# Order of VectorE's work in a 72-job dense stage: normalise early, fill the row table in the first attention, spread the kept folds

## The reference, cut to what matters

```python
x = x + attention(layernorm(x))                       # first attention
m = gelu(layernorm(x) @ w1 + b1) @ w2 + b2            # MLP
x = layernorm(x_in + x + m)
logits = einsum('bld,ed->ble', x, gate_weight)
kth_val = sort(logits.reshape(-1))[4 * 128 * 6 - 1]
gates = logits * (logits >= kth_val)
h = gelu(einsum('bld,ehd->bleh', x, w1) + b1)         # eight experts
out = einsum('blde,ble->bld', einsum('bleh,edh->blde', h, w2) + b2, gates)
x = layernorm(x + out)
```

## Time and profile before

| | |
|---|---|
| time, median of 3 runs | 1162.04 us (1162.0 to 1164.67) |
| profiled execution | 1153.58 us |
| its span, first to last instruction | 1151.9 us |
| mean granted TensorE clock | 0.922 |
| TensorE busy | 962.3 us, 84% |
| VectorE busy | 863.6 us, 75% |
| ScalarE busy | 741.1 us, 64% |
| GpSimd busy | 406.5 us, 35% |

### The profile page before, as it was taken

One profiled execution on the slowest core, in us unless ns is written; L12 is line 12 of the kernel. 1 busy time (PEld: TensorE's weight loads), 2 busy tenths in 40 slices (PEclk: granted clock), 3 DMA queues, 4 the chain that ended last, 5 costly groups with the idle time before them and its releaser, 6 DMA issues. The chain is left out here.

```text
span 1151.9 us, 29135 instructions
## 1 busy us (share of the span) xinstructions
PE 962.3 (84%) x10214; PEld 611.6 (53%) x10214; DVE 863.6 (75%) x2339; ACT 741.1 (64%) x1409; POOL 406.5 (35%) x572
## 2 busy tenths in 40 slices
PE   3999999946788999949889999589888861899995
PEld 2788887733444444414334444256565541689852
DVE  2899898836569999549899877558999864688833
ACT  2666666637688888828676788346555530688834
POOL 3455455434443000000100100113676677366643
PEclk9999999978799999979999999769989875899998
DMA  4000000010002999863222110100111101233244
GB/s 128 4 3 3 4 3 3 4 58 0 1 19 74 174 170 166 163 164 97 75 86 87 55 49 17 57 22 28 32 47 48 46 23 48 77 88 83 76 108 131
DMA packets 87997, 72.61 MB, mean 63 GB/s; under 512 B 8994, under 2 KB 73764, under 8 KB 87856
## 3 DMA queue, kind: packets, MB, share of 16 engines
q1 hardware_dynamic: 79088, 60.05, 23.1%
q0 software_dynamic: 4544, 8.60, 2.3%
q10 hardware_dynamic: 4224, 2.10, 0.7%
HBM read 40.14 MB, written 31.49 MB: 62 GB/s over the span
## 5 line engine op out<-in xcount | busy, mean ns | idle before, releaser
L778 ACT ACTIVATE d__hf<-d__HB,d__d 128x512 f32<-128x512 f32 x288 | 185.8, 681 | 76.2 <-PE d__HB L1001 72.1
L839 DVE TENSOR_TENSOR d__hl<-d__hf,d__hh 128x1024 f16<-128x1024 f32 x144 | 175.6, 1224 | 30.8 <-ACT d__hh L783 28.7
L783 ACT ACTIVATE d__hh<-d__hf 128x1024 f16<-128x1024 f32 x144 | 152.2, 1057 | 4.6
L751 POOL TENSOR_SCALAR d__rstd<-d__mv 128x4 f32<-128x4 f32 x16 | 15.0, 937 | 383.8 <-DVE d__mv L953 383.8
L999 PE MATMUL d__YB<-d__hh,d__w2h 128*128 128x512 f16 x288 | 110.3, 383 | 30.7 <-DVE d__hl L839 30.7
L999 PE MATMUL d__HB<-d__xh,d__w1h 128*128 128x512 f16 x288 | 114.2, 396 | 0.0
L1000 PE MATMUL d__HB<-d__xl,d__w1h 128*128 128x512 f16 x288 | 114.1, 396 | 0.0
L1001 PE MATMUL d__HB<-d__xh,d__w1l 128*128 128x512 f16 x288 | 113.1, 393 | 0.0
L1001 PE MATMUL d__YB<-d__hh,d__w2l 128*128 128x512 f16 x288 | 110.4, 383 | 0.0
L1000 PE MATMUL d__YB<-d__hl,d__w2h 128*128 128x512 f16 x288 | 110.3, 383 | 0.0
L298 POOL TENSOR_SCALAR_AFFINE_SELECT a__pt<-a__pt 128x512 f32<-128x512 f32 x128 | 81.6, 661 | 71.7 <-ACT a__pt L341 71.5
(11 more groups left out here) (376 smaller groups left out, 2532.9 us busy)
## 6 DMA issues: line engine op xcount, KB each, us to landing
rows<-d__blank SPq DMA_DIRECT2D x72, 268.0 KB, 7.6
d__G<-gates SPq DMA_DIRECT2D x64, 256.0 KB, 3.1
c__xin<-rows SPq DMA_DIRECT2D x39, 134.0 KB, 2.2
d__stage<-e_w SPq DMA_DIRECT2D x16, 256.0 KB, 3.2
b__stage<-e_w SPq DMA_DIRECT2D x32, 128.0 KB, 2.2
c__yb<-parts SPq DMA_DIRECT2D x8, 256.0 KB, 8.3
c__yb<-parts ACTq DMA_DIRECT2D x8, 256.0 KB, 8.8
out<-c__xo SPq DMA_DIRECT2D x8, 256.0 KB, 2.3
```

What stands on the lines that cost most here:

```text
L778: act.activation(hf[:, q, f], HB[:, f], gelu, scale=1.0 / WS, bias=b1[:, at:at + 1]).then_inc(s_["h_free"], 1)
L783: act.activation(hh[:, q, f - 1:f + 1], hf[:, q, f - 1:f + 1], ACT.Copy).then_inc(s_["hi_done"], 1)
L839: dve.tensor_tensor(hl[:, q, f], hf[:, q, f], hh[:, q, f], ALU.subtract).then_inc(s_["lo%d_done" % i], 1)
```

## The change

Three edits. (1) On VectorE in the dense stage hn(s+3) moves to the second place of the step, ahead of low(s,1), the statistics of job s+4 go ahead of xa, the first low weights go from step -4 to step -3 together with b2s and its wait for the small load. (2) The 72 writes of blank rows move to SP's queue in the first attention, five after each of its normalised blocks, from a tile with four rows for each partition instead of one row read four times. (3) The 22 kept results are folded at intervals of 9/5 steps, in steps 31 to 68, and each chunk has a sum of its own (eight tiles, not four).

```diff
@@ attention_0
+        blank = m.sb("blank", [P, 4, ROW])
+        blanks = rows.rearrange("(i p r) c -> p i r c", p=P, r=4)
...
             sp.dma_start(x[:, 4:NT, :], d["x"][:, 4:NT, :]).then_inc(x_rest, 16)
+            sp.wait_ge(blank_set, 1)
+            for i in range(BLANKS * NC_):
+                if i % 5 == 0:
+                    sp.wait_ge(hn_done, i // 5 + 1)
+                sp.dma_start(blanks[:, i], blank[:]).then_inc(blanked, 16)
+            sp.wait_ge(blanked, 16 * BLANKS * NC_)
...
             pool.wait_ge(cleared, 4)
+            pool.memset(blank[:], BLANK).then_inc(blank_set, 1)
             pool.wait_ge(loaded, 16 * LOADS)
@@ raw_pair(s)
-    i = s - FOLD_0
-    return M_JOBS + i if i >= 0 and kept_raw(M_JOBS + i) else None
+    for j in range(M_JOBS, FOLD_0):
+        if kept_raw(j) and FOLD_0 + (j - M_JOBS) * 9 // 5 == s:
+            return j
+    return None
@@ dense_0
-        acc = m.sb("acc", [P, 4, CT])
+        acc = m.sb("acc", [P, NC_, CT])
-        blank = m.sb("blank", [P, 1, ROW])
@@ dense_0, sync
-            sp.wait_ge(s_["blank_set"], 1)
-            for i in range(BLANKS * NC_):
-                if i % 4 == 0:
-                    sp.wait_ge(s_["counted"], min(i // 4 + 1, ROUNDS + 2))
-                sp.dma_start(blanks[:, i], blank[:].to_broadcast([P, 4, ROW])).then_inc(s_["blanked"], 16)
             sp.wait_ge(s_["gt_done"], 1)
@@ dense_0, vector
-            dve.wait_ge(s_["loaded"], 16)
-            dve.tensor_scalar(b2s[:], b2, WS, None, ALU.mult).then_inc(s_["b2_done"], 1)
...
+                c = s + 3
+                if 0 <= c < M_JOBS:
+                    if c:
+                        right_full(dve, "lift", c - 1)
+                    dve.wait_ge(s_["rstd0_done"], c + 1)
+                    for a in range(4):
+                        ins = dve.tensor_scalar(hn[:, a, :], x1[:, 4 * c + a, :], mv0[:, a, 0:1], rstd0[:, a:a + 1],
+                                                ALU.subtract, ALU.mult)
+                        ins.then_inc(s_["hn_done"], 1) if a == 3 else first.inc(ins)
                 if 0 <= s < JOBS:
                     low(s, 1)
...
                     left_full(dve, *post)
+                    wait(dve, s_["xn_done"], closed)
...
                 if 0 <= s + 1 < JOBS:
                     low(s + 1, 0)
-                if post:
-                    (the wait for rstd_done and xa)
-                c = s + 3
-                (hn(s + 3), as above)
                 c = s + 4
                 (statistics of job s + 4)
+                if post:
+                    (the wait for rstd_done and xa)
-                if s == BEGIN or 0 <= s - 5 < E:
-                    j = 0 if s == BEGIN else s - 4
+                if s == BEGIN + 1 or 0 <= s - 5 < E:
+                    j = 0 if s == BEGIN + 1 else s - 4
...
                     ins.then_inc(s_["w_done"], 1)
+                    if j == 0:
+                        dve.wait_ge(s_["loaded"], 16)
+                        dve.tensor_scalar(b2s[:], b2, WS, None, ALU.mult).then_inc(s_["b2_done"], 1)
```

## The result

The changed kernel took 1117.41 us (median of 4 runs, 1115.49 to 1118.96) beside 1162.3 for the kernel before in the same rounds (4 runs, 1162.0 to 1164.67): ratio 0.9623, 95% interval 0.959 to 0.9656. The forecast was 1121.2, in a range of 1111 to 1136. The profiled execution took 1118.96 us with a span of 1117.2, against 1153.58 and 1151.9 before. Some executions of a kernel fall into a slower group; ratios here compare the faster ones alone.

What follows compares the result with a forecast made beforehand. Bound taken: TensorE's own work plus three dense-stage losses (start and normalisation steps, one long stall, chunk-closing steps). Gains 17.0 + 19.8 + 4 = 40.8 us, then 0.7% from profile to median, gave 1121.2 us, range 1111 to 1136.

Steps and rivals of the forecast that it cites:

- Start and early steps: Dense stage up to job 7's first matmul: reordering VectorE's normalisation work gains 17.0 us, bounds 12 to 19.2.
- A(1): Start of L953, the bn_aggr of the job leaving the pipeline, in dense-stage step 1: forecast at 279.0.
- The loop: Dense-stage steps 2 to 4, from one bn_aggr start to the next: 9.85 us a step, with 0.83 for hn held.
- The end of 12 us: Lower bound of the early-step gain: two GpSimd xl instructions hold hn, or the lower clock hits a step without slack.
- Step 5: Early dense-stage step without hn: forecast 7.5 us.
- The stall: Wait before the first fold, gates queued behind SP's table writes: 24.94 us becomes 5.18, gain 19.8; 16 if landing takes twice as long.
- Rival 3: The stall at the first fold stays because gates to G is slow by itself: total gain 21.0, 1141; chance 0.04.
- The folds: Dense-stage steps 33 to 70: spreading kept folds cuts closing-step losses from 21.9 to 17.8 us; gain 4, bounds 0 and 9.
- the prediction's signs of being wrong: Attention ending after 250, early steps over 11 us, or the low clock coming back in the fold steps.
- Rival 2: Spread folds pile up at steps 57 to 59 and 65 to 69, fourth part loses 4: 1129.2; chance 0.1.
- The row table in the first attention: 72 writes, 19.8 MB, issued by SP on idle DMA engines: no effect taken; bounds -1 to +5 us.
- Rival 4: Slower than before: the table's writes slow the first attention, decisive from 40.8 us on; at 50% 1181; chance 0.03.

Runs made afterwards that it cites:

- after: The changed kernel with all three edits, as first measured and profiled: 1117.41 us, ratio 0.9623 to the kernel before.
- norm_table: The changed kernel without the third edit (first and second edits, folds one a step as before): 1116.83 us, ratio 0.967.
- table_only: The kernel before with only the second edit, the 72 row-table writes in the first attention: 1134.25 us, ratio 0.9823.
- norm_only: The kernel before with only the first edit, VectorE's new order; old table and folds: 1138.84 us, ratio 0.9879.
- after_third: The changed kernel, unedited, run again on the third chip: 1113.95 us, ratio 0.9674 to the kernel before.
- pool_waits: The changed kernel with GpSimd's two xl subtractions waiting until the next job's hn is done; second chip: 1146.64 us, ratio 0.9665.
- after_again: The changed kernel, unedited, run again on the second chip: 1151.2 us, ratio 0.9708 to the kernel before.
- low_first: The changed kernel with low(s,1) put ahead of hn(s+3) on VectorE; second chip: 1141.11 us, ratio 0.9654.
- waits_apart: The changed kernel with GpSimd's xl waiting for hn and kept folds neither in nor directly ahead of closing steps; third chip: 1103.62 us, ratio 0.955.
- apart: The changed kernel with the 22 kept folds moved out of the closing steps, these at least four apart; second chip: 1141.82 us, ratio 0.964.
- before_again: The kernel before, unedited, sent as an experiment on the third chip: 1150.37 us, ratio 0.9971.
- fold_only: The kernel before with only the third edit, kept folds every 9/5 steps and eight sums: 1149.71 us, ratio 0.9965.
- all_three: The changed kernel with xl waiting for hn, kept folds off closing steps, and low(s,1) ahead of hn(s+3); third chip: 1097.62 us, ratio 0.9513.

## Why the prediction was right

**Start and early steps: 17.0 forecast, 14.3 and 15.8 measured** (from the attention's end to job 7, in the two pairs of before and after; norm_table against table_only gives 16.7). The mechanism is right: norm_only shows it alone. A part of the gain comes through the clock: from job 0 to job 7 TensorE's own busy time fell by 4.8 us in the first pair and by 9.4 in the other (56.87 to 47.45), because less of it was at 1.2 GHz; no run separates this from the waits. The losses within it, in the first pair: *A(1)* was 283.17 and not 279.0. Of that the attention's later end is 2.3; hn(1), held by L749, 0.75; GpSimd's rstd0 under the second half of the low weights (L991) about 0.4 (its two instructions took 0.43 and 1.33). The rest, 0.7, is about what after has over after_third from job 0's first matmul to A(1), 0.8 us, and after alone was at 1.2 GHz there from 272.5 to 279.3. The rows:

```profile
258.12 1.15 POOL L749 TENSOR_TENSOR d__xl<-d__h,d__xh 128x512 f16<-128x512 f32 x1
258.26 1.86 DVE L931 TENSOR_SCALAR d__hn<-dense__x,d__mv,d__rstd 128x128 f32<-128x128 f32 x4 [0.90 <-POOL d__rstd L763]
```

*The loop* was 10.02 us for 9.85, two errors that nearly cancel: hn was held by both of GpSimd's instructions (2.73 us where I had 1.03 + 0.83), while L762 took 0.28 from start to start where I had 1.05 (0.19 us beside L982, a tensor_scalar; its counterpart for the other norm stood beside L840, with two inputs from SBUF, and took 0.96). The end of 12 us given for "two GpSimd xl instructions in a row hold it" was too far down for this reason. *Step 5*: xa was held by both as well, 8.35 us instead of 7.5:

```profile
315.27 1.16 POOL L767 TENSOR_TENSOR d__xl<-d__xT,d__xh 128x512 f16<-128x512 f32 x1
315.33 2.80 DVE L982 TENSOR_SCALAR keep__xa<-d__r,d__mv,d__rstd 128x128 f32<-128x128 f32 x4 [1.18 <-POOL d__rstd L755]
316.38 1.15 POOL L749 TENSOR_TENSOR d__xl<-d__h,d__xh 128x512 f16<-128x512 f32 x1
```

So the open question of the prediction, what two GpSimd instructions in a row do, has its answer: 1.12 us alone (pool_waits), 1.86 beside one, 2.73 and 2.80 beside two. The Trainium skill (SBUF — State Buffer, "SBUF: two separate sides") says of the port pair that, of GpSimd and a VectorE instruction in a 2-port mode or with two inputs from SBUF, whoever starts first has it for the whole instruction. The trace agrees: of the four short instructions of hn at 297.12 the first ends 0.08 us after L767, the second 0.08 us after L749, and the last two take their usual 0.33; and each way round the one that came second was the longer one (2.00 for 1.16 in pool_waits). That hn runs in such a mode is not shown by itself.

**The stall: 19.8 forecast, 19.8 and 20.1 measured** (steps 31 and 32). I had kept 7.5 us from the gates' issue to the first G as the dear end; with an empty queue it was 1.84. Nothing hung on it, since the fold stood 4.5 us behind anyway. That the queue of SP was the cause is shown from both sides: with the table where it was (norm_only) the wait was 18.93 us, and table_only alone took it away. Rival 3 is out.

**The folds: 4 forecast, 0.8 and 2.3 measured.** Over all profiles, kernels with the old list took 218.1 to 219.4 us in the steps 33 to 70 (five of them, mean 218.7), those with the spread one 215.0 to 217.9 (six, mean 216.1): 2.6 us. That is not all VectorE's: with the old list each of the five had 6.8 us at 1.2 GHz in these steps, with the spread one it was 6.8, 3.4, 3.4 and in three of them none. The mechanism is right and the term was mis-sized at two closing steps. Losses measured in after, forecast in brackets: 41: 2.35 (2.5), 44: 1.9 (1.9), 49: 2.5 (2.4), 57: 0.9 (1.1), 59: 7.5 (5.6 with the clock), 65: 2.35 (2.3), 69: 3.6 (2.0). Step 59 in the timeline of after:

```profile
627.15 0.69 DVE L956 TENSOR_TENSOR d__r<-d__PB,keep__xa 128x512 f32<-128x512 f32 x1
...
631.56 1.11 DVE L982 TENSOR_SCALAR keep__xa<-d__r,d__mv,d__rstd 128x128 f32<-128x128 f32 x4 [1.18 <-POOL d__rstd L755]
632.59 0.68 DVE L894 TENSOR_TENSOR d__tmp<-dense__xs,d__G 128x512 f32<-128x512 f32 x1
...
634.03 1.23 DVE L840 TENSOR_TENSOR d__hl<-d__hf,d__hh 128x1024 f16<-128x1024 f32 x1
635.31 0.61 PE L1005 MATMUL d__YB<-d__hh,d__w2h 128*128 128x512 f16 x1 [3.33 <-DVE d__hl L840]
```

r starts 5.5 us into the step that began at 621.63, so 2.3 later than the 3.2 of a step on time, and the forecast had 2.4. TensorE then waits 3.33 us for L840, and the matmul behind it is already at the lower clock, 1.2 GHz (0.61 us for 0.39), which lasts from 634.3 to 641.1. In after_again, low_first and pool_waits, where the clock didn't fall, the same steps lose 4.6 us, just the forecast's figure without the clock. So what was mis-sized at 59 is the term for the clock: 1 us in the sum, 2.9 measured here, 1.5 in after_third, nothing in these three. The other miss is at 69, and it is the same in all six profiles with the spread list: the sum counted the wait in step 70 and not the one behind it, for the low part of job 71, where TensorE has no up products left to cover VectorE's lag:

```profile
694.37 0.39 PE L1005 MATMUL d__YB<-d__hh,d__w2h 128*128 128x512 f16 x1 [1.45 <-DVE d__hl L840]
...
697.22 0.38 PE L1005 MATMUL d__YB<-d__hh,d__w2h 128*128 128x512 f16 x1 [1.38 <-DVE d__hl L840]
```

Without the clock's fall the steps 33 to 70 were 215.0, 3.7 less than before, where the clock fell twice. Of the prediction's signs of being wrong, this one did show: the lower clock came back in the fold steps. Rival 2's pile-up is there too, at 59, but the fourth part stayed a gain in the profiles. In my expectation of waits_apart another step failed: I charged a closing step for the kept fold in it or next to it, and not for the lag with which VectorE arrives from further back. With the folds taken out of the closing steps the stage did become 208.1.

**The row table in the first attention: 0 forecast, 0 measured.** L401, the counterpart of L391 before, in the stretch 29 to 228 us, beside DMA engines at a share of 0.25, where the kernel before has 0.01 in the same stretch (its instructions alone):

```profile
29.00:228.00 199.00, 78.40 (x123) 1.00 0.25 89
```

That is 0.637 us each, and 0.634 before. A block of this attention took 13.41 us after and 13.42 before. The Trainium skill says in the same section that engine ports and those of the DMA can't slow each other; here the trace agrees on the engines' side, at 89 GB/s. Rival 4 is out: table_only is 21 us faster.

**What was not in the sum.** The attention ended at 249.6, past 247.3, because TensorE was granted 1.2 GHz from 228 to 245 us, although it had been busy 16.7 of the 18 us ahead of it (stretches of after):

```profile
210.00:228.00 18.00, 16.74 (x455) 13.43 (x453) 13.84 (x34) 11.17 (x22) 7.49 (x13) 1.00 0.02 5
228.00:245.00 17.00, 16.05 (x298) 12.85 (x299) 4.40 (x13) 7.91 (x16) 6.98 (x12) 0.50 0.01 2
```

The late end is in after, after_again, table_only, norm_only, norm_table, pool_waits, apart and waits_apart, and not in before, before_again, fold_only, low_first, all_three and after_third. It comes and goes with the same kernel, and norm_only, which has no writes there, has it too, so it isn't the table's; it is worth 2 to 4 us. What brings it on stays open. In after_again it came at 250.7, past the 250 that the prediction gave as a sign of being wrong.

**From the profile to the median.** The profiled execution took 1118.96 us where the sum gave 1112.8, 6.2 more: 2.3 in the attention, 2.7 in the start and the early steps, 3.2 in the folds, less 2.1 in the rest. By my step of 0.7% from profile to median that would have been 1127, and the median was 1117.41. So that step failed, and it happened to make up for the other misses. One profiled execution of 1153.58 had stood for a median of 1162, while the kernel before spread over 14 us on one chip (1144.37 to 1158.62); why the timed difference of the result is 10 us more than the profiled one stays open. On the third chip the medians give 40.3 us and the spans 37.6, for a sum of 40.8.

Also open is the last stage, 451 to 457 us in the four profiles of the second chip and 418 to 422 in all others: the change doesn't reach it.

## What to carry to other kernels

Before an engine's work is moved, write down what the neighbour on the shared ports will run at that time, and how many instructions in a row; making the engine off the path wait was worth 4.8 us here, where another exchange in the order of the one on it (low_first) was worth 0.7. A small transfer behind a long queue costs the whole queue, so fill tables where the issuing engine and the DMA engines are idle. When work is spread over steps, keep account of an engine's lag from step to step: here a lag went down by 1.3 us in a step at most, and 2.3 us of it at step 59, on top of the fold there, made TensorE wait 3.33.

## What the runs showed of the hardware

- Four short VectorE instructions took 1.12 us alone, 1.86 beside one GpSimd instruction of 1.15, and 2.73 to 2.81 beside two in a row: one of the four was held by each. GpSimd's own took 1.16, and 2.00 when it started 0.23 us behind a VectorE low part of 1.22.
- TensorE went down to 1.2 GHz in a stretch that it was 94% busy in, behind one of 93%, with 298 matmuls recorded in 17 us; after_third, the same kernel, was at 1.2 GHz for 3.4 us there and ended this stage 2.1 us earlier.
- The write of the gates with nothing ahead of it in its queue let the first read be asked for after 1.84 us; 6.9 and 7.5 with the table's writes ahead of it.
- 19.8 MB written during the first attention, at some 100 GB/s, left VectorE's and TensorE's pace there as it was (13.41 us a block, 13.42 before).
